# Decoder block with routed experts on one core: the final loads wait for the results of the tiles that hold tokens

## What is computed

```python
logits = jnp.einsum('th,eh->te', x, router_weight)
gate = jax.nn.softmax(logits, axis=-1)
top_probs, top_idx = jax.lax.top_k(gate, TOP_K)               # TOP_K = 2 of 8 experts
h_mid = jax.nn.gelu(jnp.einsum('th,ehf->etf', x, moe_w1))
expert_out = jnp.einsum('etf,efh->eth', h_mid, moe_w2)
moe_out = jnp.einsum('eth,et->th', expert_out, weights)       # weights: the two kept gates
return hidden_after_attn + moe_out                            # then residual + layer norm: the output
```

## Time and profile before

| | us |
|---|---|
| three runs, median | 768.32 (767.08 to 770.19) |
| the profiled execution's own time | 771.22 |
| its span, first to last instruction | 769.4 |
| TensorE busy (matmuls) | 651.1 |
| VectorE busy | 528.0 |
| ScalarE busy | 388.7 |
| GpSimd busy | 311.3 |
| mean granted TensorE clock | 0.926 of full speed |

### The profile page before, as it was taken

The page is one execution under the profiler, slowest core; times in us unless marked ns, Lnnn a source line. Parts: engine busy times, 40 slices in busy tenths (PEclk is TensorE's granted clock), DMA queues, the critical chain, the costliest instruction groups (busy, mean ns, idle before and its releaser), DMA issues.

```text
span 769.4 us, 19214 instructions
## 1 busy us (share of the span) xinstructions
PE 651.1 (85%) x5188; PEld 543.0 (71%) x5189; DVE 528.0 (69%) x1846; ACT 388.7 (51%) x921; POOL 311.3 (40%) x439
## 2 busy tenths in 40 slices
PE   6799999999844889898876329999999999999790
PEld 4679898998723667676655217888888888888340
DVE  2368778878834668787875747777777777777373
ACT  1446565666436566555343614555555555555044
POOL 0246777777550022655668732222222222222132
PEclk9999999999976999989976559999999999999996
DMA  6343443443310000111111322222222222221584
GB/s 202 98 129 100 142 121 101 142 132 83 95 26 16 2 3 2 51 50 58 57 50 68 114 90 65 69 70 81 69 73 78 69 79 73 69 82 56 167 355 154
DMA packets 47709, 68.13 MB, mean 89 GB/s; under 512 B 10576, under 2 KB 34512, under 8 KB 47664
## 3 DMA queue, kind: packets, MB, share of 16 engines
q1 hardware_dynamic: 39080, 46.01, 20.3%
q0 software_dynamic: 6480, 17.87, 6.2%
q10 hardware_dynamic: 2104, 3.68, 1.5%
HBM read 40.21 MB, written 23.12 MB: 82 GB/s over the span
## 4 chain that ended last, share of the span: by engine, by line
PE 33%; issue 28%; DVE 3%; DMA 2%; SPq 1%; ACT 1%; ACTq 0%; DVEq 0%; POOLq 0%
PE half_bank L145 9%; PE half_bank L147 9%; PE half_bank L146 9%; PE half_bank L1920 5%; PE half_bank L1901 2%; DVE region_en_small L155 1%; DMA region_y_rows<-results 1%; DVE region_y_rows L1664 1%; ACT all_w L1678 1%; SPq L1708 1%; DVE all_w L921 1%; DMA results<-all_w_qkv,ex_home 0%; SPq L1707 0%; DVE region_en_small L158 0%; DMA all_xh<-dispatched 0%
## 5 line engine op out<-in xcount | busy, mean ns | idle before, releaser
L1739 POOL DMA_INDIRECT results<-all_w_qkv,ex_home x71 | 68.2, 960 | 201.5 <-DVE all_w_qkv L1864 177.1
L1772 ACT ACTIVATE region_hid_hi<-half_bank 128x256 fp32r<-128x256 f32 x142 | 46.7, 381 | 81.0 <-PE half_bank L1920 81.0
L969 POOL DMA_INDIRECT dispatched<-all_xh,all_slot_u x64 | 67.9, 1062 | 40.2 <-DVE all_slot_u L1341 23.3
L145 PE MATMUL half_bank<-region_w_hi,region_hid_hi 128*128 x284 | 81.4, 287 | 2.5 <-DVE region_hid_lo L1856 2.5
L146 PE MATMUL half_bank<-all_w,region_hid_hi 128*128 x284 | 79.7, 281 | 0.0
L147 PE MATMUL half_bank<-region_w_hi,region_hid_lo 128*128 x284 | 79.5, 280 | 0.0
L1864 DVE TENSOR_SCALAR all_w_qkv<-half_bank,ex_gate 128x256 f32<-128x256 f32 x71 | 34.3, 484 | 49.1 <-PE half_bank L147 48.5
L1759 ACT ACTIVATE all_xh<-half_bank,all_ln_b,all_ln_w 128x128 f32<-128x128 f32 x142 | 57.7, 467 | 18.8 <-PE half_bank L1901 18.8
L145 PE MATMUL half_bank<-region_w_hi,region_x_hi 128*128 x142 | 62.5, 440 | 0.5 <-DVE region_x_lo L1849 0.5
L145 PEld LDWEIGHTS half_bank<-region_w_hi,region_hid_hi 128*128 128x128 f32 x284 | 53.2, 187 | 13.4 <-issue 10.4
L1766 ACT ACTIVATE all_w_proj<-half_bank 128x512 f32<-128x512 f32 x71 | 42.5, 599 | 39.1 <-PE half_bank L147 39.1
(11 more groups left out here) (247 smaller groups left out, 1805.6 us busy)
## 6 DMA issues: line engine op xcount, KB each, us to landing
all_xh<-dispatched SPq DMA_DIRECT2D x71, 130.5 KB
all_w<-in_moe_w_dram SPq DMA_DIRECT2D x32, 256.0 KB, 3.1
region_y_rows<-results SPq DMA_DIRECT2D x12, 512.0 KB, 10.4
all_resid<-at_x SPq DMA_DIRECT2D x32, 128.5 KB
shared_x_t<-in_x_t_dram SPq DMA_DIRECT2D x16, 256.0 KB, 4.2
at_x_tok<-in_x_dram SPq DMA_DIRECT2D x16, 256.0 KB, 4.3
region_y_rows<-results SPq DMA_DIRECT2D x8, 256.0 KB, 9.5
out_dram<-all_w ACTq DMA_DIRECT2D x4, 512.0 KB
```

The costliest lines, as they stand in the source:

```text
L145: nc.tensor.matmul(out, a_hi, b_hi, start=(start and i == 0), stop=False)
L969: nc.gpsimd.indirect_dma_start(out=dram["dispatched"], out_offset=bass.IndirectOffsetOnAxis(ap=keep["slot_u"][g % SENDS][:, u, k:k + 1], a ...
L1739: nc.gpsimd.indirect_dma_start(out=dram["results"], out_offset=bass.IndirectOffsetOnAxis(ap=home[par][:, 0:1], axis=0), in_=ym[par], in_of ...
L1772: nc.scalar.activation(hid_hi[par][:, cs, :], p_t[half], ACT.Copy).then_inc(s["hid_high"], 1)
```

## The change

Four edits, all in `experts`:

1. `results_of_real_tiles`, behind the table on VectorE: takes the last entry of `up_to` (the number of tiles that hold tokens), halves it by a shift, and writes 16 times the number of even and of odd tiles that hold tokens to `landed_i`; then `table_ready` goes to 2.
2. `end_sync` loads these two numbers into registers and waits for `ym_out[par]` to reach them (at least 16), in place of the count of all 71. The wait for all stands at SP's very end.
3. `y_rows` becomes a function over three places: tiles 0 to 27 of the first results at 0 to 28 KB and of the second at 32 to 60 KB, so that the high weights of expert 7 (28 to 32 KB and 60 to 64 KB), which the empty tiles use, stay; tiles 28 to 31 of both go over the low w1 weights of experts 0 and 1 (`y_last`).
4. `end_tensor` issues only the residual of turn 0 ahead of the first wait, and then one turn ahead.

```diff
@@ -1538,6 +1538,7 @@
     n_tiles, up_to, before = m.sb("n_tiles", [P, E]), m.sb("up_to", [P, E]), m.sb("before", [P, E])
     tail_row, tail_i = m.sb("tail_row", [P, E]), m.sb("tail_i", [P, E], I32)
     count_i, tiles_i = m.sb("count_i", [P, E], I32), m.sb("tiles_i", [P, E], I32)
+    half_i, half_f, landed_i = m.sb("half_i", [P, 1], I32), m.sb("half_f", [P, 2]), m.sb("landed_i", [P, 2], I32)
     place, xh2 = keep["place"], [rows[:, :, :].rearrange("p u d -> p (u d)") for rows in keep["xh2"]]
     wide, tables = place("wide", 68, [P, MOE_TILES, E]), place("tables", 70.25, [P, 6, MOE_TILES])
     hot_t, en_small = place("hot_t", 72, [P, MOE_TILES, E]), place("en_small", 74.25, [P, 22 * 4])
@@ -1577,7 +1578,15 @@
     WIDEST = 4
     TURNS = [(0, 2), (2, 2)] + [(first, WIDEST) for first in range(4, TILES - 4, WIDEST)] + [(TILES - 4, 2), (TILES - 2, 2)]
     SHARED = 4
-    y_rows = place("y_rows", 0, [P, 2, TILES, D])
+    FULL = TILES * (E - 1) // E
+    y_first = [place(f"y_first{i}", 32 * i, [P, FULL, D]) for i in range(2)]
+    y_last = w1[:, 0:4, :].rearrange("p (i a) (b d) -> p i (a b) d", i=2, d=D)
+
+    def y_rows(i, first, wide):
+
+        assert first >= FULL or first + wide <= FULL
+        return y_first[i][:, first:first + wide, :] if first < FULL else y_last[:, i, first - FULL:first - FULL + wide, :]
+
     out_rows = w2[:, :, :]
     en_stats, en_mv = ([part(en_small, first + i * WIDEST * k, WIDEST, k) for i in range(2)]
                        for first, k in ((0, 6), (12 * WIDEST, 2)))
@@ -1595,14 +1604,22 @@
         eng.dma_start(dram["out_group"][:, :, tiles, :], out_rows[:, tiles, :]).then_inc(out_stored, 16)
 
     def end_sync(sp):
+        sp.wait_ge(s["table_ready"], 2)
+        landed = [sp.alloc_register(f"landed{par}") for par in range(2)]
         for par in range(2):
-            sp.wait_ge(ym_out[par], 16 * (LAST // 2 + 1 - par))
+            counted = sp.alloc_register(f"counted{par}")
+            sp.reg_load(counted, landed_i[0:1, par:par + 1])
+            sp.reg_alu(landed[par], counted, 16, ALU.max)
+        for par in range(2):
+            sp.wait_ge(ym_out[par], landed[par])
         for j, (first, wide) in enumerate(TURNS):
             for k in range(2):
-                sp.dma_start(y_rows[:, k, first:first + wide, :], dram["results_of"][k][:, first:first + wide, :])\
+                sp.dma_start(y_rows(k, first, wide), dram["results_of"][k][:, first:first + wide, :])\
                   .then_inc(y_in[j], 16)
         for j in range(SHARED + 1, len(TURNS), 2):
             store(sp, j)
+        for par in range(2):
+            sp.wait_ge(ym_out[par], 16 * (LAST // 2 + 1 - par))
 
     def end_tensor(pe):
 
@@ -1613,22 +1630,21 @@
             return keep["banks"][2 * (j % SETS) + h][:, :]
 
         def pair_of(j, h):
-            return slice(TURNS[j][0] + 2 * h, TURNS[j][0] + 2 * h + 2)
+            return TURNS[j][0] + 2 * h, 2
 
         def residual(j):
             wait(pe, sum_read, j - SETS + 1)
             for h in range(TURNS[j][1] // 2):
-                nc.tensor.matmul(sums(j, h), const["identity"][:, :], keep["resid"][:, pair_of(j, h), 0:D], start=True, stop=False)
-
-        for j in range(SETS - 1):
-            residual(j)
+                nc.tensor.matmul(sums(j, h), const["identity"][:, :], keep["resid"][:, slice(pair_of(j, h)[0], sum(pair_of(j, h))), 0:D], start=True, stop=False)
+
+        residual(0)
         for j in range(len(TURNS)):
             pe.wait_ge(y_in[j], 32)
             for h in range(TURNS[j][1] // 2):
-                ins = nc.tensor.matmul(sums(j, h), const["identity"][:, :], y_rows[:, 0, pair_of(j, h), :], start=False, stop=True)
+                ins = nc.tensor.matmul(sums(j, h), const["identity"][:, :], y_rows(0, *pair_of(j, h)), start=False, stop=True)
             ins.then_inc(sum_mm, 1)
-            if j + SETS - 1 < len(TURNS):
-                residual(j + SETS - 1)
+            if j + 1 < len(TURNS):
+                residual(j + 1)
 
     def end_pool(pool):
         for j, (first, wide) in enumerate(TURNS):
@@ -1655,7 +1671,7 @@
         dve.wait_ge(keep["keep_done"], GROUPS * 2)
         for j, (first, wide) in enumerate(TURNS):
             par = j % 2
-            rows, more = (y_rows[:, i, first:first + wide, :] for i in range(2))
+            rows, more = (y_rows(i, first, wide) for i in range(2))
             dve.wait_ge(y_in[j], 32)
             dve.wait_ge(sum_mm, j + 1)
             for h in range(wide // 2):
@@ -1675,7 +1691,7 @@
             par = j % 2
             act.wait_ge(shift_ready, j + 1)
             for t in range(wide):
-                ins = nc.scalar.activation(out_rows[:, first + t, :], y_rows[:, 0, first + t, :], ACT.Identity,
+                ins = nc.scalar.activation(out_rows[:, first + t, :], y_rows(0, first + t, 1)[:, 0, :], ACT.Identity,
                                            bias=en_shift[par][:, t:t + 1], scale=en_rstd[par][:, t:t + 1])
             ins.then_inc(out_ready, 1)
             if j < SHARED or j % 2 == 0:
@@ -1821,7 +1837,18 @@
             steps.mark(V.tensor_copy(expert_i[:, :], expert_f[:, :]))
             V.tensor_copy(first_i[:, :], row_at[:, :]).then_inc(s["table_ready"], 1)
 
+        def results_of_real_tiles():
+
+            real = up_to[:, E - 1:E]
+            steps.chain(V.tensor_copy(half_i[:, :], real))
+            steps.chain(V.tensor_scalar(half_i[:, :], half_i[:, :], 1, None, ALU.logical_shift_right))
+            steps.chain(V.tensor_copy(half_f[:, 1:2], half_i[:, :]))
+            steps.chain(V.tensor_tensor(half_f[:, 0:1], real, half_f[:, 1:2], ALU.subtract))
+            steps.chain(V.tensor_scalar(half_f[:, :], half_f[:, :], 16.0, None, ALU.mult))
+            V.tensor_copy(landed_i[:, :], half_f[:, :]).then_inc(s["table_ready"], 1)
+
         tile_table()
+        results_of_real_tiles()
         for e in range(1, E // 2):
             weights.make_low(dve, "w2", e)
 
```

## The result

The changed kernel took **764.30 us**, median of six runs (761.52 to 768.66); the kernel before took 768.59 beside it. The ratio is 0.9945 (95% interval 0.9921 to 0.9968): faster, by 4.2 us and not by 9.0, and 0.3 us above the range I gave. Four more comparisons of the same kernel gave 0.9923, 0.9905, 0.9932 and 0.9935; the mean of the five is 0.9928, 5.5 us. So the sign was right and the size was not. One of the 42 executions of the changed kernel, at 1321 us, is left out of its ratio.

A forecast was written before the change was run, and what follows sets the result against it. The ending's loads were taken to wait at SP for all 71 scatters, though only 68 tiles hold tokens. Loads start 9.9 us earlier, the end moves 8.6 to 9.3, taken 9.0: 768.3 - 9.0 = 759.3 us, range 756.8 to 764.0.

The forecast's parts named there:

- The wait ends 9.9 us earlier: SP's wait before the ending's loads ends at tile 67's landing, so loads start at 711.1 instead of 720.98.
- I take L near 4 us, cost nothing: Scatters of empty tiles 68 to 70, issued beside the ending's loads, land in about 4 us and delay nothing.
- L: Time an empty tile's scatter takes to land beside the ending's loads; up to 5.1 us was to cost VectorE nothing.
- second rival: Empty tiles' scatters wait partly behind loads, landing in 10.4 us and holding GpSimd's ending: 765.8 us, chance 0.05.
- The queue rows: ScalarE's queue moved 0.52 MB beside SP's 7.99 MB, taken to show scatters on a second queue get their turn.
- TensorE's start and turns: TensorE's ending starts at 717.85; turn 2's sum comes at 723.0, 8.8 us earlier; then 3.44 us a turn.
- One turn ahead: TensorE's first sum stands behind two residual instructions instead of three turns' residuals; turn 2's sum behind 12, at 723.0.
- Half of the engines work on the stores and are behind all the time: In the ending, DMA share 0.50 was read as a store backlog, 0.93 MB, falling by 0.2 MB without vanishing.
- The sign that I had named: A DMA share below 0.5 between the last loads and 753 would mean that the stores drained.
- two ways to count the end: Span's end: if stores stay behind, 9.3 us earlier; if they drain, it follows the last issue, 8.6 us; 9.0 taken.
- About 4 us less behind the last one: In the second rival, no store backlog remains, so the span ends about 4 us sooner behind VectorE's last turn.
- The six small operations: On VectorE behind the table, 1.2 to 1.5 us, hidden by its later 7.64 us wait for the first rows.

The follow-up runs named there:

- e1: The changed kernel, but SP waits for all 71 scatters before the ending's loads; ratio to the kernel before 0.9994.
- c1 to c4: Four repeats of the changed kernel without any edit, run beside other versions; ratios to the kernel before 0.9923, 0.9935, 0.9905 and 0.9932.
- e3: The changed kernel without the scatter of empty tile 70 alone, those of tiles 68 and 69 kept; ratio to the kernel before 0.989.
- e4: The changed kernel with TensorE's old order, residuals of three turns ahead of the first result; ratio to the kernel before 0.9948.
- e2: The changed kernel without the scatters of the three empty tiles 68 to 70 and the waits on them; ratio to the kernel before 0.9905.
- e8: The same kernel as e2, run again beside a repeat of the changed kernel; ratio to the kernel before 0.9882, time 753.83 us.
- c4: The changed kernel a fifth time, without any edit; ratio to the kernel before 0.9932.
- f3: The changed kernel with the ending's reciprocal root moved from GpSimd to ScalarE and VectorE, and all ten stores issued by GpSimd; ratio to the kernel before 0.9943.
- c1: The changed kernel a second time, without any edit; ratio to the kernel before 0.9923.

## Why the prediction was wrong

- **The wait ends 9.9 us earlier: right.** 711.1 said, 711.34 found; behind tile 67's scatter it is 10.1 us earlier, and e1 shows that without this start there is no gain.
- **"I take L near 4 us, cost nothing": this step failed.** Beside the loads the scatter of tile 68 takes 6.25 us from issue to the VectorE operation that waits for it (4.5 to 6.1 in c1 to c4), and from tile 69's issue to tile 70's there are 6.6 to 8.2 us, in place of 2.4 to 2.7 and 3.2. L under 5.1 us covers tile 68 alone, and there the argument held (e3). For tile 70 I had no bound at all, though I wrote down that GpSimd issues it before its ending: two landings stand ahead of it, so L counts twice. With the second rival's own formula, 715.1 + 2 x 7.2 = 729.5, turn 2 is met at 729.96. It was the rival with 0.05; the mechanism was there, at L = 7.2 and not 10.4. Its price was not: at L = 7.2 its sum, 2L - 23.3, is 8.9 us gained, as much as the forecast. 4 of these are the shorter tail, which did not come; without them it is 4.9, where the first profile has 4.6 at the last rows.
- **The queue rows did not bear what I hung on them.** That a second queue moves bytes beside SP's says that it gets a share, not how soon a single transfer lands.
- **TensorE's start and turns: right but for 1 us.** Its first residual starts at 719.35, 10.49 behind tile 67 in place of 9.43, for the home that waits. Turn 2's sum has no wait for loads, as forecast. Without the empty scatters the last rows move by 8.45 us (8.6 forecast).
- **"One turn ahead": right in the sum, wrong later.** I counted turn 2's sum behind 12 instructions. When I wrote e4's expectation I took it for nothing, with VectorE the slower; behind 20 instructions it is 1.7 us of the last rows.
- **"Half of the engines work on the stores and are behind all the time": a share of 0.5 does not show that.** I had read it out of the share. The sign that I had named, a share of 0.00, came in the first profile of after (at 739) and not in c1 to c4, e2, e3 and e8, where it stays near 0.5 (0.23 for one microsecond in c4) until 1 to 3 us ahead of the end. But at about that share the stores of the kernel before moved very different amounts (the last number is GB/s):

```profile
748.00:751.00 3.00, 3.00 (x7) 0.97 (x6) 2.74 (x12) 1.78 (x5) 1.04 (x1) 1.00 0.52 210
757.00:760.00 3.00, 0.00 (x0) 0.00 (x0) 1.01 (x5) 2.93 (x6) 1.26 (x3) 0.50 0.48 143
760.00:763.00 3.00, 0.00 (x0) 0.00 (x0) 0.16 (x1) 1.22 (x3) 0.01 (x1) 0.50 0.51 173
763.00:766.00 3.00, 0.00 (x0) 0.00 (x0) 0.00 (x0) 0.00 (x0) 0.00 (x0) 0.50 0.50 176
766.00:769.40 3.40, 0.00 (x0) 0.00 (x0) 0.00 (x0) 0.00 (x0) 0.00 (x0) 0.50 0.30 117
```

  From 757 to 760 they move about what the turns issue, 0.52 MB every 3.44 us, 152 GB/s. An estimate from these rows: from 757 on 1.87 MB move, 1.05 MB of it is issued later (turns 7 to 9) and 0.52 MB is turn 6's, issued at 756.41; so only 0.3 MB is older, less than one store. By this estimate the stores kept up with their issue in the kernel before already, and the end follows the last issues. Of my two ways to count the end it is then the second, 8.6 us, that applies; without empty scatters the end comes 6.7 to 8.3 us earlier in the three profiles, and 8.3 us in the runs.
- **"About 4 us less behind the last one", in the second rival: refuted.** The tail is 7.0 to 9.1 us, where before and e1 have 7.5 and 8.3. The stores of turns 7 to 9 are 1.05 MB, 6.3 us at 167 GB/s, and are issued faster than that. Behind tile 67's scatter the last rows of the first profile moved by 4.6 us and the end by 2.9; in its last 2.9 us the share is 0.05, one engine's worth.
- **Catching up.** VectorE, once behind TensorE, takes a turn in 733.26 - 729.96 = 3.30 us, not 3.44, so from turn 2 to the last rows it is 27.81 us against 28.38 in e2: 0.6 us given back, as the rival had (0.5).
- **The six small operations: mis-sized, hidden.** I said 1.2 to 1.5 us. In c1 to c4 and e1 they take 1.2 to 2.1 us from the first to the last, and 5.3 us in the first profile (see the last section). Even there VectorE still had 3.10 us of idle time ahead of the first rows, where it was 7.64.

So of the 4.8 us between the 9.0 forecast and the 4.2 measured, 0.7 are the forecast's excess over the 8.3 us of e2, e3 and e8, 2.8 the difference between these and the mean of the changed kernel (1.3 where both ran side by side), and 1.3 the distance of the first comparison from that mean. The three are differences of the same means, so their sum tests nothing.

## What to carry to other kernels

When a transfer is started earlier, list every small transfer that will then run beside it, and how many of them stand in a chain on one engine: a late landing counts once for each link, and the engine's next work waits behind the last link. A queue's share of bytes under load is no price for the latency of one small transfer; with no row for that, take the chain's length times two to three landings, and give the case more than 0.05. A flat share of busy engines is not a backlog either: set the bytes still to move against the bytes still to be issued. And before crediting a drained queue with a shorter tail, look at the bytes that are issued last and at their rate.

## What the runs showed of the hardware

**A scatter beside loads.** 128 rows of 1 KB by indirect DMA took 2.4 to 2.7 us alone, and 4.5 to 6.3 us (tile 68) or 6.6 to 8.3 us up to the next one's issue (tile 69, all thirteen profiles that scatter it ahead of tile 70's with all loads early) beside the ending's loads from SP's queue, at a DMA share of 0.95 in the first profile (711.3 to 730). From profile to profile it varied by up to 1.7 us for the same tile.

**A small VectorE operation that took 2.45 us.** The timeline of VectorE in the first profile of after, the last three of the six, and of GpSimd at the same place:

```profile
444.43 0.16 DVE L1846 TENSOR_TENSOR ex_half_f<-ex_up_to,ex_half_f 128x1 f32<-128x1 f32 x1 [0.93 <-DVE ex_half_f L1845]
444.62 0.17 DVE L1847 TENSOR_SCALAR ex_half_f<-ex_half_f 128x2 f32<-128x2 f32 x1
445.85 2.45 DVE L1848 CAST ex_landed_i<-ex_half_f 128x2 int32<-128x2 f32 x1 [1.05 <-DVE ex_half_f L1847]
...
445.95 2.31 POOL L1072 TENSOR_TENSOR all_resid<-all_resid,region_h_rows 128x512 f32<-128x512 f32 x2
```

The cast of two elements ran for as long as GpSimd's addition beside it, where it takes 0.17 us in c1 to c4; from the first to the last of the six it was 442.98 to 448.30, 5.3 us. Only their place together speaks for a shared cause; it was not tested.

**Stores from GpSimd** reached 291 GB/s with all engines busy in one microsecond, where those of ScalarE and SP moved 143 to 210 in the windows above, at a share near 0.5. Over the whole stretch from 735 on it is no more: 134 GB/s in f3, 147 in c1. The Trainium skill (DMA: Bandwidth & Descriptors, section on why a DMA increments its semaphore by 16) gives eight engines for an outermost dimension of 8, with which the 0.47 to 0.50 agrees. From 735 on half of f3's packets (1005 of 1947) were under 512 B, where c1 has 64 of 1068 for the same stretch, and the span went on for 3.9 us behind the last data. The wider transfer was of no use here.
